# A pre-norm block with chunked ridge attention, rewritten as one fixed order of units per engine

## Time and profile before

| | |
|---|---|
| median of 3 runs | 1702.07 us (1680.34 to 1703.43) |
| profiled execution: span of its instructions | 1697.8 us |
| PE busy, share of the span | 1484.1 us, 87% |
| DVE busy | 966.5 us, 57% |
| ACT busy | 622.8 us, 37% |
| POOL busy | 146.6 us, 9% |
| mean granted clock of PE | 0.823 |
| moved by DMA | 138.93 MB |

### The profile page before, as it was taken

One profiled execution on the slowest core, in us unless ns is written; L12 is line 12 of the kernel. 1 busy time (PEld: TensorE's weight loads), 2 busy tenths in 40 slices (PEclk: granted clock), 3 DMA queues, 4 the chain that ended last, 5 costly groups with the idle time before them and its releaser, 6 DMA issues.

```text
span 1697.8 us, 32970 instructions
## 1 busy us (share of the span) xinstructions
PE 1484.1 (87%) x11874; PEld 1230.6 (72%) x11874; DVE 966.5 (57%) x3058; ACT 622.8 (37%) x1354; POOL 146.6 (9%) x160
## 2 busy tenths in 40 slices
PE   3998987994599997689976999999999999988887
PEld 2665655663477775579865988888888898977775
DVE  6725938999756775755789235767232222153333
ACT  4443443442144443213332333344333343333333
POOL 5410010010200102000100200000200000000000
PEclk9999996996599997556796666978777789788987
DMA  7742333324342435331215221321321232201110
GB/s 257 240 150 85 99 108 79 97 93 87 75 97 72 104 84 105 69 89 46 61 30 116 73 49 48 80 63 52 102 48 51 64 76 57 64 30 60 45 60 10
DMA packets 248931, 138.93 MB, mean 82 GB/s; under 512 B 138016, under 2 KB 234400, under 8 KB 248864
## 3 DMA queue, kind: packets, MB, share of 16 engines
q1 hardware_dynamic: 241952, 116.84, 26.5%
q0 software_dynamic: 6912, 21.24, 4.4%
HBM read 79.04 MB, written 58.98 MB: 81 GB/s over the span
## 4 chain that ended last, share of the span: by engine, by line
PE 43%; issue 37%; DVE 12%; DMA 3%; ACT 2%; POOL 1%; SPq 1%; DVEq 0%; POOLq 0%; ACTq 0%
PE bank L1267 10%; PE bank L1273 5%; DVE outer L1036 4%; DVE work L1040 3%; PE bank L1260 3%; PE bank L1483 3%; PE bank L1463 3%; PE bank L1452 3%; PE bank L1474 2%; PE bank L1419 2%; PE bank L1379 2%; PE bank L1410 2%; PE bank L1433 1%; PE bank L1401 1%; PE bank L1499 1%
## 5 line engine op out<-in xcount | busy, mean ns | idle before, releaser
L1036 DVE TENSOR_TENSOR outer<-work,prow 128x496 f32<-128x496 f32 (+1 forms) x512 | 255.3, 541 | 0.0
L1040 DVE TENSOR_TENSOR work<-work,outer 128x496 f32<-128x496 f32 (+1 forms) x512 | 248.8, 528 | 0.1
L1267 PE MATMUL bank<-wqkv,xnt 128*128 128x512 f32 x512 | 239.3, 614 | 2.8 <-ACT xnt L778 2.8
L1267 PEld LDWEIGHTS bank<-wqkv,xnt 128*128 128x128 f32 x512 | 95.3, 195 | 106.3 <-issue 102.5
L859 ACT ACTIVATE kv<-bank,b1c,alpha 128x128 f32<-128x128 f32 x256 | 96.5, 458 | 100.8 <-PE bank L1401 100.8
L1419 PE MATMUL bank<-wo,kv 128*128 128x256 f32 x512 | 125.6, 392 | 9.0 <-DVE early L1151 9.0
L1273 PEld LDWEIGHTS bank<-xnt,wqkv 128*128 128x128 f32 x1024 | 119.3, 192 | 11.8 <-issue 11.5
L1273 PE MATMUL bank<-xnt,wqkv 128*128 128x128 f32 x1024 | 121.6, 276 | 0.0
L1138 DVE TENSOR_TENSOR early<-bank,gct 128x512 f32<-128x512 f32 x32 | 22.1, 692 | 164.4 <-PE bank L1474 164.4
L1419 PEld LDWEIGHTS bank<-wo,kv 128*128 128x128 f32 x512 | 95.0, 194 | 27.7 <-issue 16.4
L1433 PE MATMUL bank<-gct,pbd 128*128 128x64 f32 x512 | 69.9, 295 | 48.1 <-DMA sbd<-inv_d 48.1
(11 more groups left out here) (147 smaller groups left out, 2390.0 us busy)
## 6 DMA issues: line engine op xcount, KB each, us to landing
q_d<-qt SPq DMA_DIRECT2D x32, 512.0 KB, 2.9
gc_d<-gc SPq DMA_DIRECT2D x32, 512.0 KB, 3.3
gct<-gc_d SPq DMA_DIRECT2D x32, 512.0 KB, 4.6
qt<-q_d SPq DMA_DIRECT2D x32, 512.0 KB
gbd<-gc_d SPq DMA_DIRECT2D x64, 128.0 KB, 4.7
early<-in_L_attn_x_dram POOLq DMA_DIRECT2D x8, 512.0 KB, 6.1
xhat_d<-early POOLq DMA_DIRECT2D x8, 512.0 KB, 3.5
res_d<-early POOLq DMA_DIRECT2D x8, 512.0 KB, 5.2
```

What stands on the lines that cost most here:

```text
L1036: V.tensor_tensor(t, src[:, 0, r0 + 1:r1 + 1].unsqueeze(2).broadcast_to([P, rows, cols]), prow[:, r0 + 1:n].unsqueeze(1).broadcast_to([P, ...
L1040: V.tensor_tensor(dst[:, r0:r1, r0:n - 1], src[:, r0 + 1:r1 + 1, r0 + 1:n], tiles[m], ALU.subtract).then_inc(swept, 1)
L1267: ins = mm(dst[:], xnt[:, par, t], wqkv[:, n // 2, t, (n % 2) * BANK:(n % 2 + 1) * BANK], start=t == 0, stop=t == KT - 1)
```

## The change

The program is written anew. Each engine runs one straight list of units in a fixed order (`PE_ORDER` and the four others); no loop is left. A unit such as `GI:5` is one kind of step for one chunk, or for two chunks (`q` counts pairs of chunks). Three one-bank buffers go round among the units in `RING`; the two-bank buffer `wide` and the one-bank buffers `small`, `sum` and `tok` are single.

- Projection: keys and values only. The queries' products are dropped, and Wq is turned once (`WQ`) and joined to the rank-8 factors (`LM`). Keys of 8 chunks are kept in SBUF, and Gram (`G`) and key-value product (`C`) are units of their own of 64 moving columns.
- Elimination: a lane is stored 64 wide, a block beside a unit matrix, and the eliminated rows are dropped at each pivot. It yields a triangular factor scaled by square roots of the pivots (POOL), and ACT turns it. Scaled factors are stored in place of inverses.
- Solve: for two chunks, head by head, with 64 by 64 (or 32-row) products, even and odd heads in different halves of the array's rows and columns: `VS`, `ST` for the complement, `X1`, `GI` for the inverse factor and the inverse, `W`, `WT` for the operator and its transpose, `Y`, `Z` for the factors.
- Application: `LM` and `R` form, for all heads of a chunk, 128 rows (16 heads of 8) times 256 columns on each side; `RP` applies the 8 by 8 inverses, `AU` adds the chunk into one 256 by 256 operator that is kept in PSUM for the whole sequence, `AT` multiplies the normalised chunk with it. The decay is put into the copies' scales.
- Feed-forward: 512 tokens at a time in fp32, each product once (`H`, `O`), the magnitudes multiplied into the signs beforehand.
- All DMAs are issued by SP, POOL issues none.

```diff
+PE_ORDER = """
+WQ:0 WQ:1 WQ:2 WQ:3 XT:0.0 XT:0.1 XT:1.0 XT:1.1 K:0.0 K:0.1 K:1.0 K:1.1 G:0 K:2.0 G:1 K:2.1 K:3.0 K:3.1 G:2
...
+GI:8 AU:15 H:2.6 W:8 AT:14 H:2.7 X1:9 WT:8 AT:15 Y:8 GI:9 O:2.0 LM:8 Z:8 O:2.1 WT:9 X1:10
...
+WT:11 H:3.4 H:3.5 W:11 H:3.6 H:3.7 Y:11 O:3.0 LM:11 X1:12 O:3.1 GI:12 Z:11 W:12 X1:13 WT:12 R:11 GI:13 Y:12
+WT:13 Z:12 LM:12 X1:14 W:13 R:12 GI:14 Y:13 RP:16 LM:13 RP:17 AU:16 WT:14 Z:13 AU:17 AT:16 RP:18 W:14 RP:19
...
+H:7.0 H:7.1 H:7.2 H:7.3 H:7.4 H:7.5 H:7.6 H:7.7 O:7.0 O:7.1
+"""
...
+            def load_cross(q):
+                for k in range(2):
+                    sp.wait_ge(cross_stored[k], 16 * (q + 1))
+                if q:
+                    computed(sp, "W", q - 1)
+                    computed(sp, "WT", q - 1)
...
+                load(c2.rearrange("p u h n -> p (u h) n"), c_d[2 * q:2 * q + 2].rearrange(
+                    "c h r n -> r (c h) n")).then_inc(cross_loaded, 16)
...
+            def pivot(n, k):
+                a, r = ax[:, n % 2], rd[:, n % 2, k:k + 1]
+                at = note(V.reciprocal(r, a[:, k, k:k + 1]))
+                dve.wait_ge(swept, at)
+                parts = [(k + 1, 16), (16, HALF)] if k < 15 else [(k + 1, HALF)] if k < HALF - 1 else []
...
+                for r0, r1 in parts:
+                    rows, cols = r1 - r0, HALF + k + 1 - r0
...
+                    at = note(V.scalar_tensor_tensor(
+                        out=t, in0=a[:, k, r0:r1].unsqueeze(2).broadcast_to([P, rows, cols]), scalar=r,
+                        in1=a[:, k, r0:HALF + k + 1].unsqueeze(1).broadcast_to([P, rows, cols]),
+                        op0=ALU.mult, op1=ALU.mult))
...
+                    ends.append(note(V.tensor_tensor(rest, rest, t, ALU.subtract)))
...
+            def head_products(dst, done, c, other):
+                for h in range(PAIRS):
+                    for s in range(2):
+                        cols = slice(HD * (2 * h + s), HD * (2 * h + s + 1))
+                        ins = mm(dst[half(s), HD * h:HD * (h + 1)], key_places[c % 8][:, cols], other[:, cols],
+                                 start=True, stop=True)
...
+            def heads(dst, done, size, left, right_of):
+                for u in range(2):
+                    for h in range(PAIRS):
+                        for s in range(2):
+                            at = size * (PAIRS * u + h)
+                            ins = mm(dst[half(s), at:at + size], left(s, u, h), right_of(s, u, h), start=True, stop=True)
+                ins.then_inc(done, 1)
...
+            def complement(q):
...
+                for u in range(2):
+                    mm(by_head(dst[:])[:, u, :, 0:HALF], take[:], bd[:, q % 2, u], start=True, stop=False, skip_group_check=True)
...
+                            both = xx[half(s, HALF), q % 2, u, h]
+                            ins = mm(dst[half(s), at:at + HD], both[:, HALF:3 * HALF], both[:, HD:P], start=False, stop=True, skip_group_check=True)
...
+            def inverse(q):
+                dst, done = begin("GI", q)
+                copied(pe, "X1", q)
+                pe.wait_ge(factor_loaded, 32 * (q + 1))
+                heads(dst, done, HD, lambda s, u, h: xf[half(s), u, h], lambda s, u, h: xf[half(s), u, h])
...
+            def left_out(q):
...
+                            mm(dst[rows, at:at + DM], yp[:, u, h], wqt[:, h], start=odd == 0, stop=odd == 1,
+                               skip_group_check=True, tile_position=(0, 32 * f))
...
+            def applied(c):
...
+                for f in range(4):
+                    rows = slice(32 * f, 32 * (f + 1))
+                    ins = mm(dst[rows, 0:DM], mb[rows, c % CPB], ra[rows, n, u], start=True, stop=True,
+                             tile_position=(32 * f, 32 * f))
...
+            def operator(c):
...
+                for t in range(KT):
+                    ins = mm(dst[:, DM * t:DM * (t + 1)], la[:, n, u, P * t:P * (t + 1)], rp[:, c % 2],
+                             start=c % CPB == 0 and t == 0, stop=c % CPB == CPB - 1, skip_group_check=True)
...
+            def hidden(g, t):
...
+                for k in range(KT):
+                    ins = mm(dst[:], s1t[:, k, P * t:P * (t + 1)], y3t[:, k], start=k == 0, stop=k == KT - 1)
...
+            def output(g, h):
...
+                mm(dst[:], first_row[:], b2r[:].rearrange("p k d -> p (k d)"), start=True, stop=False, skip_group_check=True)
+                for k in range(2):
...
+                    for t in range(FT):
+                        copied(pe, "H", g, t)
+                        ins = mm(dst[:, DM * k:DM * (k + 1)], hid[:, t, at:at + P], s2t[:, t], start=False,
+                                 stop=t == FT - 1, skip_group_check=True)
```

More of the change, by code:

```diff
@@ L24 @@
 BANK = 512
+GROUP = 4
+GROUPS = NCH // GROUP
+TWOS = NCH // 2
 RIDGE, LN_EPS, SCALE, DECAY = 1e-4, 1e-5, 0.125, 0.9
[L27 to L77, removed]
+PASSES = [(0, 0), (0, 1), (1, 0), (0, 2), (1, 1), (0, 3), (1, 2), (1, 3)]
@@ L102, in build, with sb @@
+    r_d = scratch("r_d", [NCH, P, DM])
+    minv_d = scratch("minv_d", [NCH, P, 32])
+    place, uses, ringed = {}, {}, 0
+    for unit in steps(PE_ORDER):
+        if unit[0] in RING:
+            where, ringed = ringed % 3, ringed + 1
+        else:
+            where = "wide" if unit[0] in WIDE else "small" if unit[0] in SMALL else "sum" if unit[0] == "AU" else "tok"
+        place[unit] = (where, uses.get(where, 0))
+        uses[where] = uses.get(where, 0) + 1
     with ExitStack() as ctx:
-        def sb(name, shape, dt=F32):
-            return ctx.enter_context(nc.sbuf_tensor(name, shape, dt))
+        def sb(name, shape):
+            return ctx.enter_context(nc.sbuf_tensor(name, shape, F32))
@@ L160, in build @@
[L160 to L176, removed]
@@ L279, in build, with ps @@
-        o_ready, scaled, o_done = sem("o_ready"), sem("scaled"), sem("o_done")
+        def ps(name, size):
+            return ctx.enter_context(nc.psum_tensor(name, [P, size], F32))
+        bank = {n: ps(f"ring{n}", BANK) for n in range(3)}
+        bank["wide"] = ps("wide", 2 * BANK)
+        for name in ("small", "sum", "tok"):
+            bank[name] = ps(name, BANK)
+        filled = {n: sem(f"filled_{n}") for n in bank}
+        drained = {n: sem(f"drained_{n}") for n in bank}
+        wkv = sb("wkv", [P, 2, KT * HEADS * HD])
@@ L1218, in _ @@
[L1218 to L1229 removed]
+                    dve.wait_ge(coef_ready, g - 1)
@@ L1591, in _, with begin, turn_wq @@
-            chunk(None, None, LAST)
+            def begin(*unit):
+                where, n = place[unit]
+                pe.wait_ge(drained[where], n)
+                return bank[where], filled[where]
+            def turn_wq(i):
+                dst, done = begin("WQ", i)
+                pe.wait_ge(wq_loaded, 16)
+                pe.wait_ge(ident_set, 2)
+                for a in range(2):
+                    for t in range(KT):
+                        h = 2 * i + a
+                        ins = nc.tensor.transpose(dst[:, DM * a + P * t:DM * a + P * (t + 1)], wqn[:, t, P * h:P * (h + 1)],
+                                                  ident[:])
+                ins.then_inc(done, 1)
```

2126 lines of the change are left out of this document (882 added, 1244 removed).

## The result

The changed kernel takes **1064.91 us** (median of 4 runs, 1064.24 to 1068.12), the kernel before 1702.65 beside it: ratio **0.6305**, interval 0.6245 to 0.6365. The forecast was 1117 with a range of 980 to 1360.

The account below looks back on a forecast made before the run. PE was taken to bound the kernel: 971 us of passes at full clock, 17 start, 5 end, 60 clock and 60 waits make 1113, plus 4.3 around the span, 1117 us; range 980 to 1360.

Parts of the forecast that it names:

- the pace of the head-by-head products: PE's small products on half the array's rows or columns: 0.029 us a pass, 10,240 passes, 297 us.
- Passes at full clock: All PE passes of the new program, summed without a gap at full clock: 971 us.
- The clock: Time lost to a lowered PE clock in the small products, mostly in the last sequence: 60 us, ends 15 and 349.
- Start, end and waits: PE idle before the first projection 17 us, after the last output product 5, waiting in between 60.
- The single `wide` buffer and the operand loads: Copy hand-overs, 92 us if uncovered, and late loads for the next chunks, 0 to 117; 60 taken for all waits.
- The pinch at `X1:4`: PE has some 34 us of work while small inverses and transfers take about as much: a few us, within the waits.
- The other engines: DVE, ACT, DMA, SP and POOL: costed at nothing because PE covers them.
- Row halves in turn: Head-by-head passes on different row halves cannot overlap and cost 0.058 us: 238 us more, 1355; chance 0.11.
- Halves buy nothing: Head-by-head passes on half the rows cost as much as full 64-column products: 1820 or 2760 us; chance 0.05.
- cheaper halves: Loads of two halves run beside each other, so `VS`, `X1`, `Y`, `Z` take half: 59 us less, 1058; chance 0.06.
- The low clock: All 349 us of small products run at clock 0.50, 349 us lost in place of 60: 1406; chance 0.09.

Follow-up runs that it names:

- two half-by-half runs: Changed kernel with head-by-head, Gram and cross products issued all on one array half, then the other: 1380.17 us; Gram and cross products alone: 1109.92 us.

## Why the prediction was right, and where its sizes were off

PE's passes set the time, as forecast, and the pace of the head-by-head products is the one that was chosen. The span of 1063.1 us is 977 of passes at full clock, 26 that the clock cost while PE was busy, and 59 in which PE was idle. Laid out in the same way, the 1697.8 us of the kernel before are 1237, 247 and 214. So of the 635 us between the two spans 259 are passes, 221 the clock and 154 waits. What a single part of the rewrite gave of this was tried for the shorter elimination, the width of the hidden layer and the order of the halves; for the others it is not shown. The forecast was 52 us too high, by these terms:

- *Passes at full clock*, forecast 971, are 977: PE's 1003.7 busy less the clock's 26. That the sum comes so near is in part luck, since its terms miss both ways. `LM`, `R` and `RP` took 82 us where 111 stood: an `R` unit of 32 passes takes 1.87 (856.54), 0.058 a pass, not the 0.073 scaled from the earlier trace rows, and the small products of `LM` lie beside the large ones. The by-head units took more: 1.93 us where 64 x 0.029 = 1.86 stood (112 units), 1.08 where 0.93 stood (64 units), 18 us in all, and `ST` some 8; key and value passes took 5 more (those next to a small unit, last section), and the rest are smaller.
- *The clock*, forecast 60, is 26. Of the 39 lost in all, 13 fall while PE waits, in the start and from 480 to 520, and cost nothing more there. The other three runs of this kernel had mean clocks of 0.968 to 0.974, so the term itself moves by some 10 us. The stretches at 0.77 and 0.50 do not come back: 700 to 900, where by-head units stand thickest, has 0.99. The two half-by-half runs show why the term was uncertain: with the other order of the same products it would have been 174.
- *Start, end and waits*, forecast 17 + 5 + 60, are 59 us idle, of which the start has 21 (5.85 until Wq is there, 1.2, 12.4 and 1.6 after it). The single `wide` buffer and the operand loads, on which the 60 rested, cost little: PE idles 1.4 us for operands (`W`) and 1.1 for the copy out of `wide`. The waits stand at `RP` instead (5.9, 7.1, 3.1), which the prediction had not priced by itself. The pinch at `X1:4`, "a few us", was real: it showed as 6.8 us as soon as the wait ahead of it was taken away. Around the span the profiled execution has 1.8 us (1064.88 in all), where the prediction left 4.3.
- *The other engines.* DVE was forecast near 480 and is 476.2; a pass at about 49 us, and the first has 48.5 from its first reciprocal to its last; ACT 422 and 408.5; DMA 560 us of 16 engines and 46.0% of 1063.1, 489, with 357,792 pieces where some 300,000 stood. That the shorter elimination is hidden was tried, and held.
- *The rivals.* Row halves in turn, 1355: the price of 0.058 is what a pass behind one on the same half pays in the half-by-half order, and the kernel's own order does not pay it. The Trainium skill, "TensorEngine Tiling (Array Packing)", section Gotcha 1: PSUM Pressure, says that different row tiles cannot access one PSUM bank at the same time. Here both halves write one bank and differ in rows and columns; two passes take 1.92/32 = 0.060 us, and 64 columns at the pace of a hidden tile's pass are 0.429 x 64/512 = 0.054, so the two did not go one behind the other. Where page and trace differ, the trace decides; tiles that share their columns were not tried. "Halves buy nothing" is out by the same row, and "cheaper halves", 1058, came near in time but not by its mechanism: 8, 32 and 64 moving columns have the same pitch, 29 ns. The low clock, 1406, asked for 349 us where 26 were lost.

## What to carry to other kernels

Where PE bounds, sum its passes by their pitch from start to start, and check others only for room: 173 us more of VectorE cost nothing here, 14 us less of TensorE gave 15. Let neighbouring small products lie on different parts of the array, because the order alone decided over 314 us, by the pitch and by the clock. A wait that was removed on SP's queue, which all transfers share, came back one unit later: ask what is late next before counting it as a gain.

## What the runs showed of the hardware that was not expected

- The granted clock was 0.50 over 27.3 us in which PE was busy without a gap, with by-head units taken half by half; with the halves alternating it was 0.99 in the thickest stretch, and with half-by-half units only singly or in pairs among full products 1.00.
- A pass on 64 rows and 64 columns of the array costs 29 to 30 ns with a neighbour on the other half, for 8, 32 and 64 moving columns alike, and 48 to 52 in the mean of a unit done half by half. A Gram or cross pass, on all 128 rows and 64 columns, costs 30 and 53 within its unit. Behind a pass on its own half either kind mostly starts 58 ns later.
- A full pass next to a by-head unit hands over to its successor after 0.52 to 0.53 us, elsewhere after 0.429: four passes between two such units take 1.92 (363.89), and 4 x 0.429 is 1.72. Going from one kind to the other and back costs 0.2 us.
